# Routed feed-forward stage of a fused attention and expert layer: places given out in units of 128 in place of 256

## The chip, the cores and the metric

The kernel runs on one core of a Trainium2 chip. The metric is the device time of one execution in microseconds; every time here is of that core. PE is TensorE, DVE is VectorE, ACT is ScalarE, POOL is GpSimd, SP is SyncE, which issues most of the transfers.

## What is computed

For 4096 rows of 256 numbers (8 batches of 512), in float32:

```python
xn = layernorm(x)
attn = differential_attention(xn)        # 16 heads, two softmaxes each, output projection, layer norm
logits = xn @ switch_w + switch_b        # 8 experts
route, prob = argmax(logits), max(softmax(logits))
ffn[t] = prob[t] * (gelu(xn[t] @ w1[e] + b1[e]) @ w2[e] + b2[e])   # e = route[t], w1 256x1024, w2 1024x256
out = x + attn + ffn
```

Each row needs the feed-forward of one expert only, and how many rows an expert gets is known only on the chip.

## The kernel before

There are two stages, each a block in which every engine has its own instruction list and engines wait for each other through semaphores.

**Front stage** (`front_stage`, lines 109 to 1100). After the layer norm, 64 pairs of heads (8 batches times 8 pairs) are worked through in 512 steps of 8 to a pair: scores on PE, maximum on DVE (L872), exponential on ACT (L621), scaling on POOL (L468), combination on DVE (L839), transposes (L1012) and the product with V (L1027) on PE. The switch logits come out beside the V projections.

**Routing.** The generator `routing` (from L700) holds the plan as 27 small DVE operations; `ROUTE_OPS` says how many are slipped in behind each step from step 452. They find each row's expert, count the rows of each expert, and give every row a place: an expert gets whole tiles of 256 places (`FFN_TILE`). So 23 tiles (5888 places) cover every way in which 4096 rows can fall to 8 experts. L751 to L767 turn counts into tiles, the end of each expert's tiles (`tile_end`) and its first place (`base`); L789 to L799 say which expert each tile has (`tile_expert`). Places are turned into a table place to token with one-hot matrices: 24 of 32 are made by POOL (one to a step from step 476), 8 by DVE (one every third step), and 32 small matmuls (L1040) in the last pair join them. Places that no row holds get token 0 and are computed too.

**Feed-forward and output stage** (`ffn_and_output_stage`, from L1144). Matrices are split into a high and a low part, and each product is three matmuls (`THREE`) on operands of type float32r. Every engine goes through 23 turns, one for each tile n: turns 0 to 2 unrolled, 18 in a hardware loop, 2 unrolled (`turns`). Turn n:
- PE (`body`, L1668): the hidden layer of tile n, 48 matmuls with w1 as weights and 256 places moving (L1647), in four groups of 12; 4 transposes of tile n+1 (L1633); then the output of tile n-1, 48 matmuls (L1662), in which 128 places are the weights and the 256 columns of w2 move, once for each half of the tile.
- ACT (L1425): for each of the four groups two Gelus (L1435) and a copy as high part (L1438); the high part of tile n+1's rows (L1422); the high part of w2 (L1445).
- DVE (L1505): the low part of each group (L1522), among them the high part (L1490, two halves) and the low part (L1494, two halves) of w1 for tile n+1; the low part of tile n+1's rows (L1482); bias and eviction of tile n-1's output (L1502).
- POOL (L1379): fetches the rows of tile n+2 with two indirect transfers (L1137), then the low part of w2 of tile n (L1386), which waits for ACT's high part.
- SP (L1283): loads w1 of tile n+2, w2 of tile n+1 (1 MB each, always, also if the expert is the same), their biases, and stores tile n-1's output (L1305), which waits for DVE.

PE begins the hidden layer of tile n+1 only when L1494 and L1482 for it are done (lines 1639 and 1640). For the last tile the low part of w2 is split between POOL and DVE (L1559), after DVE's eviction of the tile before. SP issues the first loads of the output stage in the last turn; the later ones stand in its list behind the wait for the last tile's store. The output stage then projects 16 groups of 256 rows (L1689), fetches each row's feed-forward result by its place (L1401, which waits for all stores), normalises and adds on DVE (L1554 to L1613), and stores.

Of the kernel before, what the change touches and what calls it, by code (L numbers as in the profile page):

```python
# [30 lines left out]
T = B * S  # L31
# [25 lines left out]
SC = SLOTS // P  # L57

# [43 lines left out]
def front_stage(nc, ins, wp_d, xn_d, oW_d, oP_d, consts, slot_u, prob, tile_expert, token, ahead, s_ost):  # L102
# [3 lines left out]
    with ExitStack() as ctx:  # L106
# [18 lines left out]
        with ExitStack() as early:  # L125
            exr, oh, inc, exc, ones, col, den, line, column, column_u, high_hot, low_hot0, marks, _, low_hot1 = (
                early.enter_context(nc.sbuf_tensor(name, shape, U32 if name == "column_u" else F32))
                for name, shape in (
# [39 lines left out]
        tiles, tile_end, base = sb("tiles", [P, NE]), sb("tile_end", [P, NE]), sb("base", [P, NE])  # L168
# [493 lines left out]
        def _(dve):  # L662
# [35 lines left out]
            def routing():  # L698
# [89 lines left out]
                fe = [P, FFN_TILES, NE]  # L788
                step(vec.tensor_tensor(past, tile_end[:, :].unsqueeze(1).to_broadcast(fe),  # L789
                                       consts[:, C_T:C_T + FFN_TILES].unsqueeze(2).to_broadcast(fe), ALU.is_le))  # L790
                yield
# [977 lines left out]
```

## Time and profile before

| what | us |
|---|---|
| runs of the kernel before: median of 3 (lowest, highest) | 1867.96 (1867.92, 1871.78) |
| profiled execution, its own time | 1870.38 |
| its span in the trace | 1868.6 |
| PE busy, of the span | 1809.5 (97%) |
| DVE busy | 1552.2 (83%) |
| ACT busy | 1416.2 (76%) |
| POOL busy | 706.8 (38%) |

Times in rows are microseconds from the start of the span unless marked ns; a line of a timeline gives the start, the time that a run of like instructions took together, the engine, the line of code, output<-inputs, the shape and the count, and in brackets the idle time of the engine before it with what ended it. "PEld" is PE's loading of weights, which overlaps its matmuls.

### The profile page before, as it was taken

To read this page: it belongs to the slowest core of one execution; us is meant where nothing else is said; L and a number is where in the kernel's file an instruction comes from. 1 tells how busy PE (TensorE), PEld (TensorE's weight loads), DVE (VectorE), ACT (ScalarE), POOL (GpSimd) and SP (SyncE) were. 2 spreads that over 40 slices of the span, in tenths; PEclk is the share of its full clock that TensorE was granted. 3 is DMA by queue.
4 is the path that set the end of the run, shared out by engine and by line. 5 is a ranking of instruction groups with operands and counts; after the bars stand their busy time and mean duration, and the time that the engine had idled before them with its cause. 6 is when DMAs were issued, how large, how long until landed. Compare 5 with 4: busy or idle time off the path is not lost. (4 is left out here: it accounts for less than half of the span.)

```text
span 1868.6 us, 33187 instructions
## 1 busy us (share of the span) xinstructions
PE 1809.5 (97%) x10656; PEld 1411.6 (76%) x10656; DVE 1552.2 (83%) x2562; ACT 1416.2 (76%) x3307; POOL 706.8 (38%) x789
## 2 busy tenths in 40 slices
PE   5899999999999999999999999999999999999896
PEld 4677777777777777777777777777777799999896
DVE  7888888888888888888888888889998776666488
ACT  6898888888888888888888888888788776666311
POOL 4444222333333222333333323232266455555443
PEclk9999999999999999999999999999999999999999
DMA  9998888888888888888888888888787686676797
GB/s 311 265 243 231 238 225 218 218 229 214 215 221 229 222 214 224 228 210 208 227 224 220 216 227 227 216 218 224 208 204 180 217 294 234 238 236 208 252 325 231
DMA packets 214133, 429.33 MB, mean 230 GB/s; under 512 B 28193, under 2 KB 108961, under 8 KB 207969
## 3 DMA queue, kind: packets, MB, share of 16 engines
q1 hardware_dynamic: 208960, 413.09, 79.6%
q0 software_dynamic: 5024, 14.42, 2.6%
q8 instruction: 74, 1.21, 0.3%
q14 instruction: 75, 0.61, 0.1%
HBM read 176.02 MB, written 50.07 MB: 121 GB/s over the span
## 5 line engine op out<-in xcount | busy, mean ns | idle before, releaser
L621 ACT ACTIVATE e<-p_score,nmax 128x512 f32<-128x512 f32 x1024 | 697.4, 689 | 129.3 <-DVE nmax L872 128.8
L872 DVE TENSOR_REDUCE nmax<-p_score 128x2 f32<-128x1024 f32 x512 | 623.8, 1218 | 168.5 <-PE p_score L1000 167.3
L468 POOL TENSOR_SCALAR e<-e,rrec,lam 128x512 f32<-128x512 f32 x512 | 394.0, 769 | 945.1 <-DVE rrec L832 944.9
L1000 PE MATMUL p_score<-ks,qs 128*128 128x512 f32 x2048 | 578.8, 404 | 8.6 <-DMA ks<-k_parts 7.6
L1000 PEld LDWEIGHTS p_score<-ks,qs 128*128 128x128 f32 x2048 | 365.1, 188 | 177.9 <-ACT e L621 52.3
L839 DVE SCALAR_TENSOR_TENSOR pm<-e,rrec 128x512 f32<-128x512 f32 x512 | 394.5, 771 | 0.4 <-POOL e L468 0.2
L963 PE MATMUL p_proj<-xh,w 128*128 128x512 f32 x1024 | 385.9, 418 | 6.0 <-POOL xl L446 4.6
L553 ACT COPY pT<-p_tr 128x512 f32<-128x512 f32 x512 | 301.1, 588 | 112.3 <-PE p_tr L1012 111.9
L1012 PEld LDWEIGHTS p_tr<-consts,pm 128*128 128x128 f32 x2048 | 249.2, 140 | 80.8 <-issue 19.5
L1012 PE MATMUL p_tr<-consts,pm 128*128 128x128 f32 x2048 | 308.3, 273 | 1.7 <-ACT pT L553 1.5
L1027 PE MATMUL p_pv<-pT,v 128*64 128x512 f32 x1024 | 247.7, 605 | 0.7 <-ACT pT L553 0.7
L963 PEld LDWEIGHTS p_proj<-xh,w 128*128 128x128 f32 x1024 | 194.3, 190 | 41.2 <-issue 6.5
L621 ACT ACTIVATION_READ_ACCUMULATOR e<-p_score,nmax 128x1 f32 x1024 | 205.9, 201 | 0.0
L963 PE MATMUL p_proj<-xl,w 128*128 128x512 f32 x512 | 202.0, 394 | 0.0
L1662 PE MATMUL p_y<-w2p,hp 128*128 128x256 f32 x1104 | 137.7, 284 | 2.6 <-DVE w2p L1559 2.6
L1386 POOL TENSOR_TENSOR w2p<-w,w2p 128x2048 fp32r<-128x2048 f32 (+1 forms) x22 | 99.6, 4526 | 106.0 <-ACT w2p L1445 106.0
L1662 PEld LDWEIGHTS p_y<-w2p,hp 128*128 128x128 f32 x1104 | 133.6, 191 | 2.8 <-DVE w2p L1559 2.8
L1027 PEld LDWEIGHTS p_pv<-pT,v 128*64 128x64 f32 x1024 | 62.1, 136 | 95.9 <-issue 95.0
L1435 ACT ACTIVATE h<-p_h,b 128x256 f32<-128x256 f32 x184 | 76.8, 468 | 75.9 <-PE p_h L1647 75.9
L1647 PE MATMUL p_h<-xsp,w1p 128*128 128x256 f32 x1104 | 130.1, 277 | 2.6 <-ACT h L1435 2.1
L1647 PEld LDWEIGHTS p_h<-xsp,w1p 128*128 128x128 f32 x1104 | 127.7, 188 | 3.6 <-ACT h L1435 2.3
L963 PEld LDWEIGHTS p_proj<-xl,w 128*128 128x128 f32 x512 | 98.0, 191 | 11.7
(177 smaller groups left out, 1863.7 us busy)
## 6 DMA issues: line engine op xcount, KB each, us to landing
ks<-k_parts SPq DMA_DIRECT2D x512, 256.0 KB, 4.6
qs<-q_parts SPq DMA_DIRECT2D x512, 128.0 KB, 4.4
w<-weight_parts_scratch SPq DMA_DIRECT2D x56, 1024.0 KB, 10.0
w<-in_w SPq DMA_DIRECT2D x46, 1024.0 KB, 7.8
oT_parts_scratch<-oT SPq DMA_DIRECT2D x32, 512.0 KB
op<-oT_parts_scratch SPq DMA_DIRECT2D x32, 512.0 KB
wv<-weight_parts_scratch SPq DMA_DIRECT2D x56, 256.0 KB, 5.4
weight_parts_scratch<-w SPq DMA_DIRECT2D x8, 1024.0 KB, 5.7
```

Of the source, the lines that this page charges most:

```text
L468: nc.gpsimd.tensor_scalar(e2, e2, rrec[:, g % 4, 1:2], lam[:, 0:1], ALU.mult, ALU.mult).then_inc(s_e2, 1)
L553: nc.scalar.copy(pT[pair % 2][st // QT][:, :, qt * P:(qt + 1) * P], p_tr[:, :, :]).then_inc(s_pT, 1)
L621: nc.scalar.activation(ex[:, g % EX, m, :], p_score[g % 2][:, m, :], ACT.Exp, bias=nmax[:, g % 2, m:m + 1], accum_out=rsum[:, g % 4, m:m + ...
L839: vec.scalar_tensor_tensor(out=pm[:, g % 4, :], in0=ex[:, g % EX, 0, :], scalar=rrec[:, g % 4, 0:1], in1=ex[:, g % EX, 1, :], op0=ALU.mult ...
L872: vec.tensor_reduce(nmax[:, g % 2, :], p_score[g % 2][:, :, :], AXX, ALU.max, negate=True).then_inc(s_max, 1)
L963: last_op = nc.tensor.matmul(bank[:, :], weights(j, a, what[0], u, k), x_part(batch, b, k, 0, S), start=(k == 0 and c == 0), stop=(k == KT ...
L1000: last_op = nc.tensor.matmul(p_score[g % 2][:, m, :], qs[j][u][:, m, qt * P:(qt + 1) * P], ks[j][u][:, m, part, :], start=(part == 0), sto ...
L1012: last_op = nc.tensor.transpose(p_tr[:, k, :], pm[:, g % 4, k * P:(k + 1) * P], ident)
L1027: last_op = nc.tensor.matmul(p_pv[u * D:(u + 1) * D, :], v[it % 2][:, k, c:c + D], pT[j][u][:, k, :], start=(k == 0), stop=(k == QT - 1))
L1386: nc.gpsimd.tensor_tensor(w2p[j][:, 1, 0:f, :], w2[j][:, 0:f, :], w2p[j][:, 0, 0:f, :].bitcast(F32), ALU.subtract).then_inc(s_w2lo, 1)
L1647: last_op = nc.tensor.matmul(p_h[g % 2][:, f % 2, :], w1p[j][:, a, k, f * P:(f + 1) * P], xsp[j][:, b, k, :], start=(k == 0 and c == 0), s ...
L1662: last_op = nc.tensor.matmul(p_y[j][:, s, :], hp[j][:, a, f, s * P:(s + 1) * P], w2p[j][:, b, f, :], start=(f == 0 and c == 0), stop=(f == ...
```

## The change

An expert now gets places in units of 128. There are 16 tiles of 256 places (`PAIR_TILES`) and 7 of 128 (`HALF_TILES`), 4992 places in all. The plan gives an expert pairs of units first, as long as there are wide tiles, and its remaining units in narrow ones; that takes 42 DVE operations in place of 27. Tiles 16 to 22 are narrow: their transposes, Gelus, splits, stores and fetches are half as wide; the hidden matmuls have 128 moving columns in place of 256, and the output matmuls are 24 in place of 48. The loop over turns runs over 10 tiles in place of 18, and the last 10 turns are unrolled in place of 2. POOL makes 20 one-hot matrices and DVE 12 (every second step from step 480). The diff, cut to its core (between the operations of the plan the lines `yield` and `ready()`, a wait for the operation before, are left out; twelve of the new ones are 8 elements wide):

```diff
-FFN_TILES = (T + NE * (FFN_TILE - 1)) // FFN_TILE
-SLOTS = FFN_TILES * FFN_TILE
+PAIR_TILES, HALF_TILES = T // FFN_TILE, NE - 1
+FFN_TILES = PAIR_TILES + HALF_TILES
+PAIR_SLOTS = PAIR_TILES * FFN_TILE
+SLOTS = PAIR_SLOTS + HALF_TILES * P
+def width(n):
+
+    return FS if n < PAIR_TILES else 1
...
-ROUTE_OPS = (1,) * 8 + (0, 0, 2) + (1,) * 17
-ONE_HOTS_FROM, HOT_FIRST = 476, 4
-POOL_HOTS = 24
+ROUTE_OPS = (1,) * 8 + (0, 0, 2, 1) + (2,) * 8 + (1,) * 6 + (2,) * 2 + (1,) * 5
+ONE_HOTS_FROM, HOT_FIRST = 480, 4
+POOL_HOTS = 20
...
-                em = [P, NE, MAXT]
-                step(vec.tensor_tensor(more, inc[:, :, NT - 1:NT].to_broadcast(em),
-                                       consts[:, C_J:C_J + MAXT].unsqueeze(1).to_broadcast(em), ALU.is_gt))
-                step(vec.tensor_reduce(tiles[:, :], more, AXX, ALU.add))
-                step(vec.tensor_tensor_scan(tile_end[:, :], ones[:, 0:NE], tiles[:, :], 0.0, ALU.mult, ALU.add))
-                step(vec.tensor_tensor(base[:, :], tile_end[:, :], tiles[:, :], ALU.subtract))
-                step(vec.tensor_scalar(base[:, :], base[:, :], float(FFN_TILE), None, ALU.mult))
-                step(vec.tensor_tensor(lg[:, :, :], lg[:, :, :], base[:, :].unsqueeze(1).to_broadcast(tne), ALU.add))
+                count = inc[:, :, NT - 1:NT]
+                dve.wait_ge(s_marks, 16)
+                eu, ep = [P, NE, NT], [P, NE, PAIR_TILES]
+                step(vec.tensor_tensor(units_of, count.to_broadcast(eu),
+                                       marks[:, M_UNIT:M_PAIR].unsqueeze(1).to_broadcast(eu), ALU.is_gt))
+                step(vec.tensor_reduce(units[:, :], units_of, AXX, ALU.add))
+                step(vec.tensor_tensor(pairs_of, count.to_broadcast(ep),
+                                       marks[:, M_PAIR:MARKS].rearrange("p (e j) -> p e j", j=PAIR_TILES), ALU.is_gt))
+                step(vec.tensor_reduce(pairs[:, :], pairs_of, AXX, ALU.add))
+                step(vec.tensor_tensor_scan(pair_end[:, :], ones[:, 0:NE], pairs[:, :], 0.0, ALU.mult, ALU.add))
+                step(vec.tensor_scalar(pair_stop[:, :], pair_end[:, :], float(PAIR_TILES), None, ALU.min))
+                step(vec.tensor_tensor(pair_base[:, :], pair_end[:, :], pairs[:, :], ALU.subtract))
+                step(vec.scalar_tensor_tensor(out=less[:, :], in0=pair_base[:, :], scalar=float(PAIR_TILES),
+                                              in1=pair_stop[:, :], op0=ALU.min, op1=ALU.subtract))
+                step(vec.scalar_tensor_tensor(out=singles[:, :], in0=less[:, :], scalar=float(FS), in1=units[:, :],
+                                              op0=ALU.mult, op1=ALU.add))
+                step(vec.tensor_scalar(singles[:, :], singles[:, :], 0.0, None, ALU.max))
+                step(vec.tensor_tensor_scan(single_end[:, :], ones[:, 0:NE], singles[:, :], 0.0, ALU.mult, ALU.add))
+                step(vec.tensor_scalar(limit[:, :], less[:, :], -float(FFN_TILE), None, ALU.mult))
+                step(vec.tensor_tensor(single_at[:, :], single_end[:, :], singles[:, :], ALU.subtract))
+                step(vec.tensor_scalar(single_at[:, :], single_at[:, :], float(P), float(PAIR_SLOTS), ALU.mult, ALU.add))
+                step(vec.tensor_tensor(single_at[:, :], single_at[:, :], limit[:, :], ALU.subtract))
+                step(vec.scalar_tensor_tensor(out=shift[:, :], in0=pair_base[:, :], scalar=float(FFN_TILE),
+                                              in1=single_at[:, :], op0=ALU.mult, op1=ALU.subtract))
+                step(vec.tensor_tensor(exr[:, :, :], lg[:, :, :], limit[:, :].unsqueeze(1).to_broadcast(tne), ALU.is_lt))
+                step(vec.tensor_tensor(exr[:, :, :], exr[:, :, :], shift[:, :].unsqueeze(1).to_broadcast(tne), ALU.mult))
+                step(vec.tensor_tensor(lg[:, :, :], lg[:, :, :], single_at[:, :].unsqueeze(1).to_broadcast(tne), ALU.add))
+                step(vec.tensor_tensor(lg[:, :, :], lg[:, :, :], exr[:, :, :], ALU.add))
...
-                if g >= ONE_HOTS_FROM and (g - ONE_HOTS_FROM) % 3 == 0:
-                    c = POOL_HOTS + (g - ONE_HOTS_FROM) // 3
+                if g >= ONE_HOTS_FROM and (g - ONE_HOTS_FROM) % 2 == 0:
+                    c = POOL_HOTS + (g - ONE_HOTS_FROM) // 2
...
+        LOOP_END = PAIR_TILES // 2 - 2
-                with engine.Fori(1, LOOPED // 2 - 1) as i:
+                with engine.Fori(1, LOOP_END) as i:
-                for n in (FFN_TILES - 2, FFN_TILES - 1):
+                for n in range(2 * LOOP_END + 1, FFN_TILES):
...
-                                    p_h[g % 2][:, f % 2, :], w1p[j][:, a, k, f * P:(f + 1) * P], xsp[j][:, b, k, :],
+                                    p_h[g % 2][:, f % 2, 0:t.fs * P], w1p[j][:, a, k, f * P:(f + 1) * P],
+                                    xsp[j][:, b, k, 0:t.fs * P],
...
-                for s in range(FS):
+                for s in range(fs):
...
-                        nc.scalar.activation(h[:, g, c, :], p_h[g % 2][:, c, :], ACT.Gelu_apprx_tanh,
+                        nc.scalar.activation(h[:, g, c, 0:t.fs * P], p_h[g % 2][:, c, 0:t.fs * P], ACT.Gelu_apprx_tanh,
...
-                    v.tensor_tensor(hp[j][:, 1, 2 * g:2 * g + 2, :], h[:, g, :, :],
+                    v.tensor_tensor(hp[j][:, 1, 2 * g:2 * g + 2, 0:t.fs * P], h[:, g, :, 0:t.fs * P],
...
-            add_b2(FFN_TILES - 1, 0, LOOPED // 2, False)
+            add_b2(FFN_TILES - 1, 0, LOOPED // 2, False, 1)
```

The loads of w1 and w2, their splits and every wait stay as they are.

## Rows read from the trace of the kernel before

**Rows 1.** Busy time by stretch: PE, PEld, DVE, ACT, POOL; clock, DMA share, GB/s.
```profile
1511.00:1738.00 227.00, 227.00 (x1952) 227.00 (x1951) 142.67 (x192) 153.64 (x273) 126.31 (x54) 1.00 0.71 236
```
**Rows 2.** The chain that ended last, one turn of the feed-forward stage.
```profile
1517.74 5.44 PE p_h L1647 x48
1523.18 0.44 PE p_x L1633 x4
1523.62 5.75 PE p_y L1662 x48
```
**Rows 3.** Timeline of PE near the end of the front stage.
```profile
1443.63 0.60 PE L1012 MATMUL p_tr<-consts,pm 128*128 128x128 f32 x4
1444.16 1.94 PE L1027 MATMUL p_pv<-pT,v 128*64 128x512 f32 x8
1447.49 1.88 PE L1040 MATMUL p_proj<-high_hot,low_hot 128*128 128x46 f32 x16
```
**Rows 4.** Timeline of ACT, DVE and POOL in the turn that begins at 1517.6.
```profile
1520.66 0.69 DVE L1522 TENSOR_TENSOR hp<-h,hp 128x512 fp32r<-128x512 f32 x1 [2.00 <-ACT hp L1438]
1521.27 0.69 DVE L1490 CAST w1p<-w 128x1024 fp32r<-128x1024 f32 x1
...
1523.32 0.83 ACT L1435 ACTIVATE h<-p_h,b 128x256 f32<-128x256 f32 x2
...
1524.06 1.22 DVE L1494 TENSOR_TENSOR w1p<-w,w1p 128x1024 fp32r<-128x1024 f32 x1
1524.18 0.62 ACT L1438 CAST hp<-h 128x512 fp32r<-128x512 f32 x1
...
1524.71 0.58 ACT L1422 CAST xsp<-p_x 128x512 fp32r<-128x512 f32 x1
1525.18 1.91 ACT L1445 CAST w2p<-w 128x2048 fp32r<-128x2048 f32 x1
1525.19 0.68 DVE L1522 TENSOR_TENSOR hp<-h,hp 128x512 fp32r<-128x512 f32 x1
1525.80 1.22 DVE L1494 TENSOR_TENSOR w1p<-w,w1p 128x1024 fp32r<-128x1024 f32 x1
1526.93 0.68 DVE L1482 TENSOR_TENSOR xsp<-p_x,xsp 128x512 fp32r<-128x512 f32 x1
1527.17 4.62 POOL L1386 TENSOR_TENSOR w2p<-w,w2p 128x2048 fp32r<-128x2048 f32 x1 [4.39 <-ACT w2p L1445]
```
**Rows 5.** Groups of DVE instructions, 1290 to 1440: busy us, mean ns.
```profile
L238 DVE TENSOR_SCALAR high_hot<-marks,column,consts 128x46 f32<-128x46 f32 x8 | 2.4, 302 | 0.0
L237 DVE TENSOR_SCALAR low_hot<-marks,line 128x128 f32<-128x128 f32 x8 | 2.2, 280 | 0.0
...
L767 DVE TENSOR_TENSOR lg<-lg,base 128x256 f32<-128x256 f32 x1 | 0.4, 418 | 0.0
...
L764 DVE TENSOR_SCALAR base<-base 128x8 f32<-128x8 f32 x1 | 0.2, 159 | 0.0
```
**Rows 6.** Timeline: DVE instructions that meet a POOL instruction.
```profile
1501.53 4.65 POOL L1386 TENSOR_TENSOR w2p<-w,w2p 128x2048 fp32r<-128x2048 f32 x1 [4.40 <-ACT w2p L1445]
...
1504.33 2.13 DVE L1543 TENSOR_SCALAR rows<-rows 128x512 f32<-128x512 f32 x1
```
**Rows 7.** Timeline of the last turn (begins 1726.8) and the start of the output stage.
```profile
1736.16 2.41 POOL L1386 TENSOR_TENSOR w2p<-w,w2p 128x1024 fp32r<-128x1024 f32 x1 [6.57 <-ACT w2p L1445]
...
1738.96 1.91 DVE L1559 TENSOR_TENSOR w2p<-w,w2p 128x1024 fp32r<-128x1024 f32 x1
...
1740.93 6.01 PE L1662 MATMUL p_y<-w2p,hp 128*128 128x256 f32 x48 [2.61 <-DVE w2p L1559]
...
1752.35 0.68 DVE L1502 TENSOR_TENSOR y<-p_y,b 128x512 f32<-128x512 f32 x1
```
**Rows 8.** Busy time of single pairs of heads: 54 (no routing) and 57.
```profile
1239.80:1261.80 22.00, 22.00 (x118) 15.94 (x117) 19.63 (x31) 18.31 (x46) 7.24 (x10) 1.00 0.92 238
...
1306.50:1330.00 23.50, 22.20 (x117) 15.94 (x115) 22.20 (x47) 18.79 (x46) 6.16 (x8) 1.00 0.76 203
```

More of the change, by code:

```diff
@@ L167, in front_stage @@
         sw, swb, weight = sb("sw", [P, KT, NE]), sb("swb", [P, NE]), sb("weight", [P, NE])
-        tiles, tile_end, base = sb("tiles", [P, NE]), sb("tile_end", [P, NE]), sb("base", [P, NE])
+        units, pairs, pair_end, pair_stop, pair_base, less, singles, single_end, limit, single_at, shift = (
+            sb(name, [P, NE]) for name in ("units", "pairs", "pair_end", "pair_stop", "pair_base", "less", "singles",
+                                           "single_end", "limit", "single_at", "shift"))
         te_f = sb("te_f", [P, FFN_TILES])
@@ L787, in routing @@
                 yield
[L788 to L791, printed above, removed]
+                for ends, a, b in ((pair_end, 0, PAIR_TILES), (single_end, PAIR_TILES, FFN_TILES)):
+                    fe = [P, b - a, NE]
+                    step(vec.tensor_tensor(past[:, a:b, :], ends[:, :].unsqueeze(1).to_broadcast(fe),
+                                           consts[:, C_T + a:C_T + b].unsqueeze(2).to_broadcast(fe), ALU.is_le))
+                    yield
                 ready()
@@ L1135, in gather @@
     def gather(self, pool, n, s):
-        c = n * FS + s
+        c = n * FS + s if n < PAIR_TILES else PAIR_TILES * (FS - 1) + n
         pool.indirect_dma_start(
@@ L1242, in __init__ @@
                 self.half_before = half - 1 if j == 0 else half
+                self.fs, self.fs_next, self.fs_before = (width(n + d) if exact else FS for d in (0, 1, -1))
             def after(self, k):
@@ L1294, in body @@
                 if t.after(1):
-                    store(n - 1, 1 - j)
+                    store(n - 1, 1 - j, t.fs_before)
                 if t.has(1):
@@ L1301, in body, with store @@
                     first_of_output()
-            def store(n, j):
+            def store(n, j, fs):
                 sp.wait_ge(s_yb, n + 1)
-                sp.dma_start(ys_v[bass.ds(n, 1)].rearrange("a p s e -> (a p) s e"), y[j][:, :, :]
-                             ).then_inc(s_st[j], 16)
+                if fs == 1:
+                    a = PAIR_SLOTS + (n - PAIR_TILES) * P
+                    sp.dma_start(ys_d[a:a + P, :], y[j][:, 0, :]).then_inc(s_st[j], 16)
+                else:
+                    sp.dma_start(ys_v[bass.ds(n, 1)].rearrange("a p s e -> (a p) s e"), y[j][:, :, :]
+                                 ).then_inc(s_st[j], 16)
             x_v = ins["x"].rearrange("(n s p) e -> n p s e", s=2, p=P)
@@ L1347, in _ @@
             load_whole(2)
-            store(FFN_TILES - 1, 0)
+            store(FFN_TILES - 1, 0, 1)
             def store_out(n):
@@ L1375, in gather @@
                 pool.wait_ge(s_tr, n - 1)
-                for s in range(FS):
+                for s in range(width(n)):
                     ahead.gather(pool, n, s)
@@ L1417, in _, with x_high @@
         def _(act):
-            def x_high(n, j, fresh):
+            def x_high(n, j, fresh, fs):
                 act.wait_ge(s_tr, n + 1)
@@ L1495, in w1_low, with add_b2 @@
                                 ALU.subtract).then_inc(s_w1lo, 1)
-            def add_b2(n, j, half, fresh):
+            def add_b2(n, j, half, fresh, fs):
                 dve.wait_ge(s_y, n + 1)
@@ L1537, in body @@
                 if t.after(1):
-                    add_b2(n - 1, 1 - j, t.half_before, not t.after(3))
+                    add_b2(n - 1, 1 - j, t.half_before, not t.after(3), t.fs_before)
             assert HG == 2 * KT
@@ L1626, in _, with transposes @@
         def _(pe):
-            def transposes(n, j, half, fresh):
-                pe.wait_ge(s_xs[j], 16 * FS * (half + 1))
+            def transposes(n, j, half, fresh, fs):
+                pe.wait_ge(s_xs[j], 16 * FS * (half + 1) if fs == FS else 16 * (PAIR_TILES // 2 * (FS - 1) + half + 1))
                 if not fresh:
@@ L1631, in transposes @@
                 for k in range(KT):
-                    for s in range(FS):
+                    for s in range(fs):
                         last_op = nc.tensor.transpose(p_x[j][:, k, s * P:(s + 1) * P],
@@ L1651, in hidden, with outputs @@
                     if g == X_AT and t.first():
-                        transposes(1, 1, 0, True)
-            def outputs(n, j, fresh):
+                        transposes(1, 1, 0, True, FS)
+            def outputs(n, j, fresh, fs):
                 pe.wait_ge(s_w2lo, n + 1)
@@ L1658, in outputs @@
                     pe.wait_ge(s_yb, n - 1)
-                for s in range(FS):
+                for s in range(fs):
                     for f in range(FT):
@@ L1669, in body @@
                 if t.has(1) and not t.first():
-                    transposes(t.n + 1, 1 - t.j, t.half_next, not t.after(1))
+                    transposes(t.n + 1, 1 - t.j, t.half_next, not t.after(1), t.fs_next)
                 if t.after(1):
-                    outputs(t.n - 1, 1 - t.j, not t.after(3))
+                    outputs(t.n - 1, 1 - t.j, not t.after(3), t.fs_before)
             turns(body)(pe)
             pe.wait_ge(s_w2lo_dve, 1)
-            outputs(FFN_TILES - 1, 0, False)
+            outputs(FFN_TILES - 1, 0, False, 1)
             pe.wait_ge(s_wohi, 4)
```

75 lines of the change are left out of this document (52 added, 23 removed).

## The prediction

> **What bounds the kernel now.** I read the busy time by stretch first. In the feed-forward stretch PE is busy in 227.0 of 227.0 us and nothing else is near it: ACT 154, DVE 143, POOL 126, the transfers 0.71 of their time, clock 1.00 [rows 1]. Then the chain of waits: a turn is PE alone, 5.44 us of hidden layer, 0.44 of transposes, 5.75 of output, in sum 11.63 [rows 2]. So work taken from PE here shortens the kernel until something else in the turn ends last, and the question is what. For that I read one turn's timeline [rows 4] and the places where DVE and POOL meet [rows 6, 7]. Last, the front stage by pairs of heads, for the longer plan [rows 8].
>
> **Part 1: PE in a narrow turn.** The output matmuls keep their shape and half of them go: 24 of 48, 5.75/2 = 2.88 us saved. Two of four transposes go: 0.22 saved [rows 2]. The hidden matmuls stay 48, with 128 columns in place of 256; today one takes 5.44/48 = 0.113. No row shows a float32r matmul of 128 columns. Bounds: half of today, 0.057, and, from the other end, the pace of plain float32 products, where 4 matmuls of 512 columns take 1.94 us (8 records), 0.24 for 128 columns [rows 3]. The nearest rows are the transposes, with 128 columns: 0.44/4 = 0.11 each [rows 2], the same in the front stage; and 16 products of only 46 columns take 1.88, 0.117 each [rows 3]: with fresh weights for each matmul, fewer columns don't get below about 0.11. I take 0.108: 48 give 5.2, a saving of 0.25. A narrow turn is then 5.2 + 0.22 + 2.88 = 8.3 us for PE, 3.3 less.
>
> **Part 2: what else must fit into it.** Times from the start of the turn's hidden layer. ACT: today two Gelus take 0.83 and the high copy 0.62, and the last copy is over at 1524.8, 7.2 after the turn's start: 5.44 of hidden layer, 0.83, 0.62 and 0.3 on the way [rows 2, 4]. Half the width takes DVE from 0.68 to 0.42 [rows 4, 5], about 1 ns a column; so the two Gelus become 0.63 and the copy 0.40. The last copy is then over at 5.2 + 0.3 + 0.63 + 0.40 = 6.5, the rows' copy at 6.8, and w2's copy, unchanged at 1.9 [rows 4], at 8.7. POOL's split of w2 (4.62 [rows 4], unchanged) can run from 8.7 to 13.3, that is to 4.6 of the next turn. Today it starts 2.0 before the turn's end and is over 2.6 into the next one, before DVE's first low part at 3.1 [rows 4].
> In a narrow turn the two meet, and rows show what a meeting costs. A DVE operation of 512 columns that started inside POOL's split took 2.13 us, until 1506.46, while the split ended at 1506.18 [rows 6]: it waited for the whole instruction. Another of 1024 took 1.91 beside POOL against 1.22 alone [rows 4, 7]. The Trainium skill (page "SBUF — State Buffer", section "Who interferes with whom") states it as a rule against such a change: DVE with two inputs in SBUF, or in a two-port mode, and GpSimd lock each other out for a whole instruction. By that rule the turn below is 9.5, without it 8.7.
> So DVE and POOL take turns. DVE's share of a narrow turn: four low parts (0.61 apart today [rows 4], 0.34 at half width), two w1 copies at 0.61 and two w1 splits at 1.13 (1524.06 to 1525.19 [rows 4]): 1.36 + 1.22 + 2.26 = 4.84. POOL's is 4.65. Sum **9.5**, against PE's 8.3. (Today 4.65 + 2.44 + 3.48 = 10.6 fits into 11.63.) PE's wait: the next hidden layer needs the split of w1 and the rows' low part, the last of DVE's list. I take 9.5 for a turn in this rhythm.
> Lower bound 8.7: no lock, DVE's list alone (last copy at 6.5, low part, split, rows' low part: 0.34 + 1.13 + 0.41 and waits). Upper bound 10.6: POOL starts before DVE's last split, so that this one waits too.
> Transfers: today 236 GB/s [rows 1] in 11.63 us are 2.74 MB a turn; the narrow store and fetch take off 0.26. That is 2.48 MB in 9.5 us, 261 GB/s, and a share of 0.71 x 2.48/2.74 x 11.63/9.5 = 0.79. SP's load of w2 for the next tile waits for POOL's split, now until 4.2 in the turn, and ACT needs it at 6.8 of the next, 12 us later; today's two loads of a turn fit into 11.63. I cost them at nothing; without this cover the turn would grow to what keeps the share under 1, 7.5 us, still less. The turns that leave the loop cost nothing either: the front stage is unrolled and PE stays busy in 22.0 of 22.0 us [rows 8].
>
> **Part 3: turns 15 to 22.** Before: 7 turns of 11.63 (15 to 21) = 81.4. After: turn 15 loses two transposes, 11.4; 16 has a narrow hidden layer but the wide output of tile 15, 5.2 + 0.22 + 5.75 = 11.2; in 17 POOL is done at 2.1 and DVE is not held up, 8.7; in 18 POOL is busy to 4.6 and DVE has 4.84 and the rows' 0.42 to go, 9.9; 19 to 21 at 9.5, 28.5. Sum 69.7, **saved 11.7**.
> Last turn: before, PE starts tile 22's output 14.1 after the turn's start (1740.93 - 1726.8) and is done at 19.9, with 2.61 of waiting for DVE's half of w2 [rows 7]. After: outputs of 21 end at 8.1; ACT's w2 copy ends at 8.4, POOL's half (2.41 [rows 7]) at 10.9, and DVE's half, two SBUF inputs, waits for it and needs 1.22: 12.1, and the output 2.88 more, 15.0. The stall grows from 2.6 to 4.0 and the whole is 4.9 shorter. The output stage behind it runs on loads that SP issues after the last store, which follows DVE's eviction at 1752.35 [rows 7], 25.6 after the turn's start; that eviction stands behind the third group's load, which waits for the same split. It moves by about 4.4. **Saved 4.4**, the smaller.
>
> **Part 4: the plan.** Removed: 0.42 + 0.16 x 3 + 0.28 x 2 = 1.5 us of DVE. Added, by size from rows 5: six of 256 columns at 0.42, two of 128 at 0.28, twelve of 8 at 0.16: 5.0. Four more one-hot matrices at 0.28 + 0.30: 2.3. Together 5.8 more on DVE over five pairs of heads. Lower bound 0: a pair without routing leaves DVE 22.0 - 19.6 = 2.4 idle. Upper bound 5.8. In the pair with the densest routing of today DVE had 2.6 us more to do and the pair took 1.5 longer, PE idle for 1.3 of it [rows 8], which holds also the waits for PE's rank matmuls. New steps hold two operations each, the second waiting for the first. I take **1.2 lost**. POOL's one-hots are four fewer, and end in the same step. DVE's wait for the marks moves up, to step 464, with the maximum L872 and so ACT's exponential behind it; their load is issued 16 steps (two pairs, 44 us) before, and I cost it at nothing.
>
> **Sum.** -11.7 - 4.4 + 1.2 = -14.9. The profiled execution took 1870.4 (span 1868.6): 1855.5. The median of the runs is 2.4 lower, 1867.96: **1853.1**.
>
> **Rivals.**
> (a) DVE and POOL don't line up as said, or the lock doesn't bind: 8.7 a turn in 18 to 21 saves 3.6 more, and the last turn 1.1: 1848. For it: DVE's first low part needs to slip past POOL's split only once. Against: rows 6.
> (b) A worse rhythm, or PE's clock: with PE waiting 1.2 us in each turn and its array half filled, the clock may go to its lower level, 1.2 GHz; then 24 output matmuls cost 2.88 more, 11.2 a turn. Either, 10.6 to 11.2 for five turns, plus a plan that costs 2 or 3: 1858 to 1863. Against: PE's clock stayed at 1.00 through the pair with 1.3 us of idling [rows 8].
> (c) Slower: a float32r matmul of 128 columns goes at the pace of float32, 0.24 each: the hidden layer takes 11.6, a narrow turn 14.7. Turns 16 to 21 then cost 6 + 5 x 3.1 = 21.5 more, the end 1.7 more, the plan 1.2: 1892. It decides from where PE's gain is used up, 21.6 us / (7 x 48) = 0.064 above today's 0.113, so 0.18 a matmul. For it: nothing in the kernel has this form under 256 columns. Against: the transposes.
> (d) The plan gives no fewer tiles: excluded, the number of turns and widths is fixed in the program.
>
> **Chances.** Forecast (1850 to 1856) 0.5, (a) 0.2, (b) 0.2, (c) 0.05, the rest (a plan or a front stage that eats the gain) 0.05. A measurement of this kernel tells about 0.2%, 3.7 us, from no change. Below 1864.2 lie the first three, nearly all of (b): faster 0.91, the same 0.03, slower 0.06. The range leaves out (c) and the end of (b): 1846.5 to 1860.
>
> **What would show it.** In the trace after, narrow hidden matmuls at 5.2 us for 48 (near 2.7: rows 3 misled; near 11: (c)); turns 19 to 21 at 9.5, with PE waiting about 1.2 for DVE's L1482 or L1494; DVE's first low part in these turns longer than 1 us, ending when POOL's split ends (if all stay near 0.42, no lock: (a)); before the last output a wait of 4; pairs 58 to 62 together about 1 us longer. Wrong in kind if PE stays without waits in narrow turns or the clock of that stretch falls below 1.

## The result and the profile after

| | median us | lowest to highest | runs |
|---|---|---|---|
| before | 1868.76 | 1867.92 to 1871.78 | 4 |
| after | 1853.72 | 1851.60 to 1859.52 | 4 |

The ratio on record is 0.9909, 95% interval 0.9891 to 0.9928; the quotient of the two medians is 0.9920, inside it. By the medians the change is 15.0 us faster, where 14.9 and 1853.1 us had been forecast. The profiled execution of the new kernel is the slowest of its four, 1859.52 us (span 1857.7), 6 us above the median. So these rows show something that not every execution has, and the agreement of the medians says nothing yet about the steps.

Line numbers have moved: the hidden layer is L1712 on PE, the transposes L1698, the output L1728; w2's low part is L1450 on POOL and its last half L1624 on DVE; DVE's low parts are L1586 (groups) and L1546 (rows), w1's copy and split L1554 and L1558, the eviction L1566; ACT's copy of w2 is L1509.

Busy time by stretch, each row about one turn, turns 16 to 22 and the last outputs (columns as in [rows 1]; the digits before DMA share and GB/s are PE's granted clock):

```profile
1659.50:1670.80 11.30, 11.30 (x100) 11.30 (x100) 6.11 (x10) 6.21 (x14) 6.41 (x3) 1.00 0.71 231
1670.80:1679.30 8.50, 8.41 (x74) 8.20 (x73) 6.15 (x11) 6.20 (x14) 2.83 (x2) 1.00 0.67 179
1679.30:1689.10 9.80, 8.71 (x75) 8.51 (x75) 7.33 (x11) 6.20 (x14) 6.47 (x3) 1.00 0.98 353
1689.10:1702.50 13.40, 13.40 (x76) 13.40 (x77) 6.73 (x10) 6.19 (x14) 6.36 (x3) 0.62 0.61 201
1702.50:1711.00 8.50, 8.44 (x75) 8.23 (x73) 6.22 (x11) 6.20 (x14) 4.15 (x2) 1.00 0.72 247
1711.00:1720.80 9.80, 8.69 (x74) 8.48 (x74) 7.33 (x11) 6.21 (x15) 5.50 (x2) 1.00 0.52 177
1720.80:1732.90 12.10, 8.55 (x73) 8.35 (x73) 6.19 (x8) 6.77 (x14) 7.55 (x3) 0.96 0.75 233
1732.90:1738.40 5.50, 5.50 (x26) 5.50 (x27) 4.35 (x2) 1.05 (x1) 5.50 (x4) 0.50 1.09 360
```

In [rows 1] PE filled its stretch. Here it is full in turn 16, lacks 1.1 us in turns 18 and 21, and in turn 19 is full again for 13.4 us with the very same work: the clock was 0.62 of full speed on average.

The chain of waits, turn 16 and parts of turns 18 and 19 (for [rows 2]):

```profile
1659.49 5.31 PE p_h L1712 x48
1664.80 0.24 PE p_x L1698 x2
1665.04 5.76 PE p_y L1728 x48
...
1682.14 0.04 DVE hp L1586
1682.18 1.95 issue
...
1686.08 0.29 DVE w1p L1558
1686.37 0.78 issue
...
1688.61 0.42 DVE xsp L1546
1689.03 0.04 issue
1689.08 8.79 PE p_h L1712 x48
1697.86 0.45 PE p_x L1698 x2
```

Before, a turn's chain was PE alone. Now turn 18's runs over DVE, and the long piece of "issue" in it, 1.95 us, lies inside DVE's L1586. The timeline says what it is (for [rows 4, 6]):

```profile
1679.32 5.58 PE L1712 MATMUL p_h<-xsp,w1p 128*128 128x128 f32 x48
1679.36 4.56 POOL L1450 TENSOR_TENSOR w2p<-w,w2p 128x2048 fp32r<-128x2048 f32 x1 [5.58 <-ACT w2p L1509]
...
1682.14 2.06 DVE L1586 TENSOR_TENSOR hp<-h,hp 128x256 fp32r<-128x256 f32 x1 [2.47 <-ACT hp L1502]
1684.73 0.41 DVE L1586 TENSOR_TENSOR hp<-h,hp 128x256 fp32r<-128x256 f32 x1
...
1688.15 4.95 POOL L1450 TENSOR_TENSOR w2p<-w,w2p 128x2048 fp32r<-128x2048 f32 x1 [3.11 <-ACT w2p L1509]
1689.08 8.79 PE L1712 MATMUL p_h<-xsp,w1p 128*128 128x128 f32 x48 [1.07 <-DVE xsp L1546]
```

POOL's split runs to 1683.92. The DVE instruction that began at 1682.14 ends at 1684.20; its like alone takes 0.41. It stood still until POOL was done, and all that follows it on DVE is late, down to the rows' low part for which PE waits 1.07 us.

The last turn (for [rows 7]; it begins at 1720.81):

```profile
1729.37 0.42 DVE L1566 TENSOR_TENSOR y<-p_y,b 128x256 f32<-128x256 f32 x1 [1.40 <-PE p_y L1728]
1729.39 2.34 POOL L1450 TENSOR_TENSOR w2p<-w,w2p 128x1024 fp32r<-128x1024 f32 x1 [4.55 <-ACT w2p L1509]
1729.71 3.10 DVE L1624 TENSOR_TENSOR w2p<-w,w2p 128x1024 fp32r<-128x1024 f32 x1
...
1732.87 5.49 PE L1728 MATMUL p_y<-w2p,hp 128*128 128x256 f32 x24 [3.54 <-DVE w2p L1624]
```

DVE's half of w2 again sits out POOL's half, and PE waits 3.54 us. The 24 outputs then take 5.49 us, at the lower level of the clock (0.50, so 1.2 GHz).

The routing, pair 57 and the sum over pairs 56 to 62 (for [rows 8]):

```profile
1307.30:1330.70 23.40, 22.13 (x117) 15.92 (x115) 22.14 (x47) 18.71 (x46) 6.15 (x8) 1.00 0.77 204
...
sum 157.20, PE 155.58 PEld 112.62 DVE 146.49 ACT 129.13 POOL 68.23; mean PE 22.23 PEld 16.09 DVE 20.93 ACT 18.45 POOL 9.75
```

The same seven pairs took 157.3 before, with 142.8 of DVE. DVE does 3.7 us more and the pairs take no longer.

### The profile page after: what moved, and what is told of

The parts are those of the page before. It is cut to its first block and busy times, and to the rows that moved or that the text cites. A ratio compares the mean times of both kernels' runs of the same rounds, so it can differ in the third digit from the quotient of the medians.

```text
span 1857.7 us, 32559 instructions
## 1 busy us (share of the span) xinstructions
PE 1795.7 (97%) x10474; PEld 1397.3 (75%) x10474; DVE 1549.6 (83%) x2585; ACT 1405.4 (76%) x3307; POOL 693.7 (37%) x774
## 5 line engine op out<-in xcount | busy, mean ns | idle before, releaser
L1450 POOL TENSOR_TENSOR w2p<-w,w2p 128x2048 fp32r<-128x2048 f32 (+1 forms) x22 | 99.9, 4542 | 107.9 <-ACT w2p L1509 107.9
L1712 PE MATMUL p_h<-xsp,w1p 128*128 128x256 f32 (+1 forms) x1104 | 134.5, 283 | 4.9 <-DVE xsp L1546 2.2
L1712 PEld LDWEIGHTS p_h<-xsp,w1p 128*128 128x128 f32 x1104 | 132.0, 195 | 6.8 <-DVE xsp L1546 3.2
L1499 ACT ACTIVATE h<-p_h,b 128x256 f32<-128x256 f32 (+1 forms) x184 | 70.9, 436 | 79.6 <-PE p_h L1712 78.7
L1728 PE MATMUL p_y<-w2p,hp 128*128 128x256 f32 x936 | 121.4, 290 | 3.5 <-DVE w2p L1624 3.5
L1728 PEld LDWEIGHTS p_y<-w2p,hp 128*128 128x128 f32 x936 | 117.2, 197 | 3.7 <-DVE w2p L1624 3.7
L1586 DVE TENSOR_TENSOR hp<-h,hp 128x512 fp32r<-128x512 f32 (+1 forms) x92 | 61.1, 668 | 55.6 <-ACT hp L1502 36.0
```

The source lines that it names most:

```text
L1450: nc.gpsimd.tensor_tensor(w2p[j][:, 1, 0:f, :], w2[j][:, 0:f, :], w2p[j][:, 0, 0:f, :].bitcast(F32), ALU.subtract).then_inc(s_w2lo, 1)
L1712: last_op = nc.tensor.matmul(p_h[g % 2][:, f % 2, 0:t.fs * P], w1p[j][:, a, k, f * P:(f + 1) * P], xsp[j][:, b, k, 0:t.fs * P], start=(k = ...
L1728: last_op = nc.tensor.matmul(p_y[j][:, s, :], hp[j][:, a, f, s * P:(s + 1) * P], w2p[j][:, b, f, :], start=(f == 0 and c == 0), stop=(f == ...
```

## The experiments

They settle three things: what the plan costs; whether it is POOL's split that holds the narrow turns above 8.7; and what turn 19's 13.3 us are. Lengths of turns below are from one start of the hidden layer to the next. The kernel before ran beside each group of experiments: its median is 1873.04 us beside experiments 1 to 4, 1866.67 beside 5 to 8 and 1866.92 beside 9 to 11. So times of different groups are compared by their ratios.

**1. The plan alone.** The new routing, but all 23 tiles computed at full width.

```diff
-                self.fs, self.fs_next, self.fs_before = (width(n + d) if exact else FS for d in (0, 1, -1))
+                self.fs, self.fs_next, self.fs_before = (FS, FS, FS)
...
-                for s in range(width(n)):
+                for s in range(FS):
```

> The longer plan and the 23 tiles of the change, with tiles 16 to 22 computed at full width: the second half of a narrow tile fetches the same rows again and is not stored. Theory (the plan hides in DVE's idle time): within 0.1% of the kernel before, turns 15 to 22 as before, 11.6 each. Rival (the plan costs what I forecast): 1.2 us longer; at the bound of all of DVE's added work on the path, 5.8 longer.

Measured: 1870.86 us against 1873.04, ratio 0.9994 (0.9981 to 1.0007). The plan costs nothing that can be told from this, at most 1.3 us (which does not exclude the 1.2 of the forecast), and the gain comes from the narrow tiles. In the trace the turns from 15 on are 11.63 to 11.70.

**2. The change again.**

> The changed kernel once more, for more rounds and a second trace. Its profiled execution was 6 us longer than its three other runs, and in its trace the clock was at its lower level for 10 us in turn 19 and again at the last output. Theory (the clock falls by chance in narrow turns, after PE has waited about 1 us for DVE): the place of the fall differs in this trace or it is missing; the time is 1851 to 1860, ratio 0.991. Rival (the slow stretch is a fixed trait of the code): the same fall in turn 19, 13.4 us for that turn.

Measured: 1855.31 us, ratio 0.9908 (0.9894 to 0.9923). Turn 19 takes 13.28 in this profile too, with the clock at its lower level from about 1692.1 on. From two profiles I took this fall for a fixed trait of the kernel. Experiment 9 shows that it isn't.

**3. Hidden matmuls of a narrow tile with 256 moving columns.** The 128 surplus columns are old numbers that nobody reads.

```diff
-                                    p_h[g % 2][:, f % 2, 0:t.fs * P], w1p[j][:, a, k, f * P:(f + 1) * P],
-                                    xsp[j][:, b, k, 0:t.fs * P],
+                                    p_h[g % 2][:, f % 2, :], w1p[j][:, a, k, f * P:(f + 1) * P],
+                                    xsp[j][:, b, k, :],
```

> The hidden matmuls of the narrow tiles get 256 moving columns back; the second 128 hold what an earlier tile left there and nothing reads their results. All else stays narrow. Theory (a matmul with fresh weights costs about 0.11 whether 128 or 256 columns move, and the turn is set by DVE and POOL): narrow turns stay at 8.5 and 9.5 to 9.8; PE's array is full again, so the clock does not fall, and the time is as the fastest runs of the changed kernel or better, ratio 0.989 to 0.991. Rival (the halved columns do bring time): 1 to 2 us slower than the changed kernel. Rival (the clock falls because PE waits, whatever the columns): a fall like that in the changed kernel.

Measured: 1853.93 us, ratio 0.9909 (0.9892 to 0.9925), the same as the change on that chip. Turns 17 to 21: 8.81, 9.83, 9.22, 9.75, 9.23. Busy time by stretch, turns 18 to 20:

```profile
1677.70:1687.50 9.80, 8.99 (x75) 8.78 (x75) 7.21 (x11) 6.21 (x14) 6.24 (x3) 1.00 0.95 366
1687.50:1696.70 9.20, 9.00 (x74) 8.80 (x74) 6.52 (x11) 6.21 (x14) 5.06 (x3) 1.00 0.74 273
1696.70:1706.50 9.80, 9.05 (x75) 8.85 (x75) 7.12 (x11) 6.21 (x14) 6.21 (x3) 1.00 0.74 247
```

PE is busy 9.0 of a turn in place of 8.7: twice the columns for 0.3 us. The turn doesn't follow, since PE isn't what it is made of. The clock stayed up in turns 16 to 21 of this one profile, which at the time looked like the work of the wide matmuls. But of this kernel's six executions one without a profile took 1860.30 us at a mean granted clock of 0.989; those of the change in which the clock fell have 0.988.

**4. A short POOL.** In tiles 16 to 21 POOL makes an eighth of w2's low part; the rest is left out. DVE and every wait stay.

```diff
-                j, f = n % 2, HALF_F if n == FFN_TILES - 1 else FT
+                j, f = n % 2, HALF_F if n == FFN_TILES - 1 else FT if n < PAIR_TILES else 1
```

> For tiles 16 to 21 POOL makes only an eighth of the low part of w2 (one of 8 slices); the rest of it is left out. Every wait stays. Theory (DVE's two-input instructions wait for POOL's whole instruction): DVE's first low part in turns 18 to 21 takes 0.42 in place of 1.5 to 2.1, PE's waits of about 1.1 us in turns 19 and 22 go, the five narrow turns 17 to 21 take 8.5 each, 2 to 3 us less in all than the changed kernel with its clock up. Rival (DVE's list is too long by itself): the turns stay at 9.5 to 9.8 and only the last stall shrinks.

Measured: 1852.60 us, ratio 0.9892 (0.9874 to 0.9910). That interval overlaps the one of the change (0.9894 to 0.9923), so what follows rests on the trace and not on the time. Turns 18 to 21 of its timeline are 8.79, 8.79, 8.79, 8.80:

```profile
1691.37 5.58 PE L1712 MATMUL p_h<-xsp,w1p 128*128 128x128 f32 x48
1691.41 0.73 POOL L1450 TENSOR_TENSOR w2p<-w,w2p 128x256 fp32r<-128x256 f32 x1 [6.94 <-ACT w2p L1509]
...
1694.20 0.43 DVE L1586 TENSOR_TENSOR hp<-h,hp 128x256 fp32r<-128x256 f32 x1 [2.47 <-ACT hp L1502]
```

POOL is out of the way 2 us before DVE's first low part, which takes 0.43 in place of 1.5 to 2.1. Without POOL on the port a narrow turn is 8.8; so the lock is what the rest of the turn is made of. The transfers, at 0.90, 0.85, 0.88 and 0.60 of their time in these four turns, hold nobody up: PE is busy 8.7 of 8.8.

**5. POOL's split in four pieces**, so that DVE can slip in between.

```diff
+                pieces = 4 if PAIR_TILES <= n < FFN_TILES - 1 else 1
+                for a in range(0, f, f // pieces):
+                    b = a + f // pieces
+                    last_op = nc.gpsimd.tensor_tensor(w2p[j][:, 1, a:b, :], w2[j][:, a:b, :],
+                                                      w2p[j][:, 0, a:b, :].bitcast(F32), ALU.subtract)
```

> POOL's low part of w2 of tiles 16 to 21 is cut into four instructions of 512 columns; the same work. Theory (DVE waits for one whole instruction at a time, and the port time of both adds up to 9.5 a turn): DVE's first low part in a late narrow turn waits for at most 1.2, but later ones wait too, so a turn stays at 9.3 to 9.8. Rival (what costs is where the one long wait falls, not the sum): the turns fall to 8.8 as with the shortened POOL instruction.

Measured: 1853.59 us against 1866.67, ratio 0.9931 (0.9908 to 0.9953). Turn 18 takes 10.04, turns 20 and 21 9.14 and 9.57, turn 19 13.30 with the clock down. Timeline, turn 18:

```profile
1678.67 5.17 POOL L1453 TENSOR_TENSOR w2p<-w,w2p 128x512 fp32r<-128x512 f32 x4 [4.86 <-ACT w2p L1513]
1681.45 1.25 DVE L1590 TENSOR_TENSOR hp<-h,hp 128x256 fp32r<-128x256 f32 x1 [2.47 <-ACT hp L1506]
1682.62 1.77 DVE L1558 CAST w1p<-w 128x1024 fp32r<-128x1024 f32 x1
```

DVE's long wait of 2.06 has become two, and POOL's four pieces wait as well (5.17 in place of 4.56). Cutting the instruction changes who waits when, not the sum. The copy waits too (1.77 against 0.68), though it reads one input.

**6. DVE makes w2's low part** in the narrow tiles: alone it needs 2.28 us for what takes POOL 4.57.

```diff
-                if n == 0:
+                if n == 0 or n >= PAIR_TILES:
                     continue
...
+                if t.exact and PAIR_TILES <= n < FFN_TILES - 1:
+                    dve.wait_ge(s_w2lo, n)
+                    dve.wait_ge(s_w2hi, n + 1)
+                    v.tensor_tensor(w2p[j][:, 1, :, :], w2[j][:, :, :], w2p[j][:, 0, :, :].bitcast(F32),
+                                    ALU.subtract).then_inc(s_w2lo, 1)
```

(and the last tile's first half behind the last turn)

> For tiles 16 to 22 DVE makes the low part of w2 in place of POOL, after the eviction in its list. DVE needs 1.13 for 1024 columns where POOL needs 2.3, so by my sum the shared port is in use 4.84 + 2.26 = 7.1 a turn in place of 9.5, and DVE 7.8 of PE's 8.3. Theory: no long low parts, turns 17 to 21 at 8.8 each, the last output starts 11.0 after turn 22's start in place of 12.1, no fall of the clock in turn 19; 3 to 6 us faster than the changed kernel, ratio 0.987 to 0.989. POOL's additions for the output stage move into turns 20 and 21 and may hold DVE up there for up to 1.2 at a time. Rival (DVE, not the port, is what the narrow turns lack): the turns stay at 9.5 or grow.

Measured: 1857.19 us, ratio 0.9953 (0.9939 to 0.9967): a miss, slower than the change by the ratios (0.9908 and 0.9927 in experiments 2 and 9). Turns 18 to 21 are 8.79, 14.19, 14.39, 8.69. Two are as forecast; the timeline shows the other two:

```profile
1693.90 6.62 DVE L1558 TENSOR_TENSOR w1p<-w,w1p 128x1024 fp32r<-128x1024 f32 x1
1694.48 4.94 POOL L1455 TENSOR_TENSOR x<-x,rows 128x512 f32<-128x512 f32 x4
...
1700.90 10.50 PE L1719 MATMUL p_h<-xsp,w1p 128*128 128x128 f32 x48 [5.50 <-DVE xsp L1546]
```

POOL's list, free of the splits, went on to the output stage: its four additions of beta, which had stood behind the last split, now ran in turn 19. One DVE split of 1.22 stood still through all four of them. The forecast had put these additions into turns 20 and 21 and allowed for a hold of 1.2 at a time. PE waited 5.50, its clock fell in that wait, at about 1699.8, and the next 48 hidden matmuls took 10.50.

**7. The same with 256 moving columns.**

> As dve_w2, with 256 moving columns in the hidden matmuls of the narrow tiles, of which the second half is not used. Theory (half-filled matmuls matter only for the clock, and with PE hardly waiting it does not fall anyway): as dve_w2 within 0.1%, each hidden layer 0.1 longer. If the clock falls in dve_w2 and not here, the columns decide.

Measured: 1857.62 us, ratio 0.9951 (0.9938 to 0.9965). Turns 18 to 21: 9.07, 14.45, 11.23, 9.07, the same accident. The clock fell here too, at about 1698.1, in the same wait: wide matmuls don't keep it up through that.

**8. Narrow and wide tiles in turn** (narrow in turns 10, 12 to 22, hidden matmuls with 256 columns), so that a wide turn covers POOL's split. The core of the edit:

```diff
-    return FS if n < PAIR_TILES else 1
+    return 1 if n >= FIRST_HALF and (n - FIRST_HALF) % 2 == 0 else FS
```

> The narrow tiles are turns 10, 12, ... 22 in place of 16 to 22, wide ones between them; POOL makes w2's low part; hidden matmuls with 256 columns. Theory (port time adds up over neighbouring turns): a narrow and a wide turn need 9.5 + 10.65 = 20.15 of the port and 20.2 of PE, so a pair takes 20.2 to 20.6 where the changed kernel takes 11.63 + 9.3 = 20.9: 2 to 4 us faster in the stretch of turns 10 to 22 than hidden256. Rival (the wide turn with a narrow output, 8.5 for PE, can't hold its own 10.65 of port time next to its neighbour): pairs of 21 or more, nothing gained.

Measured: 1857.19 us, ratio 0.9953 (0.9938 to 0.9969): nothing gained. Turns alternate between 11.95 and 9.96, 21.9 a pair:

```profile
1675.40:1687.40 12.00, 11.96 (x101) 11.96 (x102) 6.61 (x10) 6.35 (x14) 7.73 (x3) 1.00 0.64 219
1687.40:1697.40 10.00, 8.79 (x77) 8.59 (x75) 7.29 (x11) 7.61 (x14) 4.76 (x4) 1.00 0.73 265
```

A wide turn of 11.63 and a narrow one of 9.4 would make 21.0. The first kind of turn (narrow hidden layer, wide output) is PE alone. The second (wide hidden layer, narrow output) has PE busy for 8.8 of 10.0, and the timeline says what it waits for:

```profile
1690.61 0.69 DVE L1598 TENSOR_TENSOR hp<-h,hp 128x512 fp32r<-128x512 f32 x1 [2.33 <-ACT hp L1514]
...
1697.35 2.86 PE L1724 MATMUL p_h<-xsp,w1p 128*128 128x256 f32 x22 [1.21 <-DVE xsp L1558]
```

POOL's split had ended at 1689.46. From 1690.61 to 1697.30 DVE works through its list with hardly a gap, and no instruction in it takes longer than it does alone (0.69, 1.22, 0.42). So this turn's 9.96 is 3.2 us until the first low part and 6.7 of DVE's own list, and not time on the port. The rival's outcome came true, but not for the rival's reason, and the sum of port times of a pair, 20.15, was not what set its length.

The results of this kernel are wrong, so it counts for its lengths only. By its code the likely reason is this: turn 8 is still in the loop and loads w1 and b1 for turn 10 as if that were wide tile 10, so the first narrow tile gets the hidden weights of another tile. The amount of work is the same.

**9. The change a third time**, beside the two that follow.

> The change once more, on the chip of the next two. Both theories: 0.991 of the time before, turns 17 to 21 at 8.7, 9.8, 13.3, 8.7, 9.8, last outputs 12.1 after the start of turn 22.

Measured: 1853.10 us against 1866.92, ratio 0.9927 (0.9914 to 0.9941). In this profile (1852.96 us) the clock stayed up. Turns 17 to 21: 8.69, 9.77, 9.18, 9.38, 9.19. Timeline of turns 19 to 22:

```profile
1688.81 5.58 PE L1712 MATMUL p_h<-xsp,w1p 128*128 128x128 f32 x48 [1.08 <-DVE xsp L1546]
...
1697.99 5.58 PE L1712 MATMUL p_h<-xsp,w1p 128*128 128x128 f32 x48 [0.50 <-DVE xsp L1546]
1700.82 1.67 DVE L1586 TENSOR_TENSOR hp<-h,hp 128x256 fp32r<-128x256 f32 x1 [2.55 <-ACT hp L1502]
...
1707.37 5.58 PE L1712 MATMUL p_h<-xsp,w1p 128*128 128x128 f32 x48 [0.70 <-DVE xsp L1546]
...
1716.56 5.61 PE L1712 MATMUL p_h<-xsp,w1p 128*128 128x128 f32 x48 [0.51 <-DVE xsp L1546]
```

PE's wait before turn 19, 1.08, is that of the first profile to 0.01 us, and the 48 matmuls behind it take 5.58 here and 8.79 there. So the fall of the clock comes in some executions and not in others, with nothing in turns 17 and 18 to tell them apart, and costs 4.0 us over turns 19 to 21 (13.28 + 8.68 + 9.77 against 9.18 + 9.38 + 9.19). In the first profile a wait of 1.08 before turn 22 brought no fall either.

The same thing happens in turn 3, where all tiles are wide. There PE waits 2.06 to 2.09 us in the middle of the hidden layer in every profile. These are the rows of the first profile and of this one:

```profile
1509.18 4.63 PE L1712 MATMUL p_h<-xsp,w1p 128*128 128x256 f32 x24 [2.07 <-ACT h L1499]
...
1510.41 3.10 PE L1712 MATMUL p_h<-xsp,w1p 128*128 128x256 f32 x24 [2.07 <-ACT h L1499]
```

The clock falls behind this wait in 6 of the 13 profiles (experiments 1, 2, 6, 10 and 11 and the first of the change) and stays up in the other 7, the kernel before among them; the fall makes turn 3 15.6 us in place of 14.1. The first profile is 6.5 us longer than this one: 4.0 in turns 19 to 21, 1.5 in turn 3, 2.2 from the start of turn 22 to the end, less 1.2 ahead of turn 2. The first two profiles of the change have both falls and this one has neither; experiment 5 has the fall in turn 19 alone. Experiments 3 and 4 can't be read as cures of it: one profile each.

**10. DVE makes the splits, and POOL is held back.** Experiment 6 with one line more, ahead of POOL's additions of beta:

```diff
             pool.wait_ge(s_scaled, 1)
+            pool.wait_ge(s_w2lo_dve, 1)
             for n in range(R):
                 add_beta(n)
```

> GpSimd takes no w2 split from tile 16 on and is held back from its four additions of beta until the last tile's split is done, so that VectorE has the shared port to itself. Theory of the port: no turn has a long wait; turns 17 to 21 at 8.7 to 8.9 each, no fall of the clock in turn 19, last outputs 11.3 after the start of turn 22. From the turns of the two profiles the stretch is then 5 to 8 us shorter than with the change, about 1848 where the change has 1854; what the late additions of beta cost behind the last tile comes off that (at most their 4.9 us). Rival (VectorE itself becomes the bound, or the clock falls for the matmuls of 128 columns whatever waits): turns of 9.5 or more, or a turn of 13, and a time at or above the change's.

Measured: **1846.37 us** (1844.71 to 1849.41) against 1866.92, ratio **0.9887** (0.9872 to 0.9903), and 6.7 us under the change on the same chip, whose interval doesn't touch this one. Turns 17 to 21: 8.68, 8.79, 8.80, 8.79, 8.79. Busy time of turns 18 to 20, then of turn 22 and the last outputs:

```profile
1679.90:1688.70 8.80, 8.69 (x74) 8.49 (x74) 8.06 (x12) 6.21 (x14) 1.66 (x1) 1.00 0.93 325
1688.70:1697.50 8.80, 8.69 (x74) 8.48 (x74) 8.05 (x12) 6.22 (x14) 1.66 (x1) 1.00 0.84 300
1697.50:1706.30 8.80, 8.68 (x75) 8.48 (x75) 8.04 (x12) 6.21 (x14) 0.00 (x0) 1.00 0.84 290
...
1715.10:1726.40 11.30, 8.52 (x73) 8.31 (x73) 7.00 (x10) 6.78 (x14) 0.00 (x0) 1.00 0.77 234
1726.40:1729.50 3.10, 3.10 (x26) 3.10 (x27) 3.04 (x2) 1.06 (x1) 3.02 (x2) 1.00 1.01 316
```

DVE does 2.3 us more work in each turn, and the turn is shorter: PE is busy 8.7 of 8.8. The last outputs start 11.3 after their turn's start and take 3.1, the clock is up, and the late additions on POOL (6.88 us for four, beside DVE's first splits of the output stage) cost less than they free. Against the profile of experiment 9, turns 17 to 21 are 2.4 us shorter and the rest behind them 2.1, in sum 4.5. The 5 to 8 that were forecast for the stretch had been counted from two profiles with the fall in turn 19; against those the turns are 6.3 shorter. In the profiles the span is 3.6 shorter, since this one has the fall in turn 3. The medians say 6.7.

**11. The same with 256 moving columns.**

> The same with 256 moving columns in the hidden matmuls of the narrow tiles. Theory of the port: turns at 8.8 to 9.1, so 0 to 2 us above the kernel with 128 columns. If the clock needs the wide matmuls also where nobody waits, this one is faster than the one with 128 columns by 3 us or more.

Measured: 1849.83 us, ratio 0.9906 (0.9891 to 0.9921). Turns 18 to 21: 9.07, 9.06, 9.07, 8.90. The median is 3.5 us above experiment 10 where 0 to 2 were expected, but the intervals overlap and the profiles' spans differ by 0.9 only. Turns 17 to 21 together are 1.0 longer, and the last outputs 1.5, where this profile has a fall of the clock after PE's wait of 2.78 and that of experiment 10 has none after the same wait. Nothing speaks for the wide matmuls here.

## Why the prediction came out right, step by step

- **Narrow hidden layer, 5.2.** Right: 5.31 in the chain of turn 16. The row that carried it was the 46-column matmul at 0.117 each: half the columns save 2%, and rival (c), which needed 0.18 a matmul, falls. Outputs at half, 2.9, and transposes at 0.24: right.
- **DVE and POOL take turns, 9.5.** Right in mechanism and size. The Trainium skill's rule (page "SBUF — State Buffer", section "Who interferes with whom") is what the rows show: DVE's first low part takes 1.5 to 2.1 and ends just behind POOL's split, and with POOL shortened (experiment 4) the turn is 8.8. A lock for one whole instruction doesn't cover experiment 6, where a DVE split recorded ahead of POOL's first addition sat out all four. Turns 17 to 21 were forecast at 8.7, 9.9, 9.5, 9.5, 9.5, and in the undisturbed profile are 8.69, 9.77, 9.18, 9.38, 9.19. The mean of the last three is 9.25: the sum of port times was 0.25 too high. In turn 20 POOL's split takes 4.56 where 4.65 was put in, DVE's share from the end of that split (1702.21) to the end of its last w1 split (1706.98) is 4.77 where 4.84 was, and POOL's next split is recorded from 1706.83, 0.15 ahead of that end. PE's waits are 0.5 to 1.1 where about 1.2 was said.
- **Rival (a), no lock,** is refuted by experiments 4 and 10, which have that length of turn, 8.8, only where POOL is off the port.
- **Rival (b), the clock.** Priced at 0.2 and for five turns, it happens in part: in two of three profiles for one turn, 4.0 us each time. The argument against it, that the clock stayed up through 1.3 us of idling in the front stage [rows 8], didn't bear that weight. The forecast had named a clock below 1 in this stretch as a sign that it is wrong in kind; by that sign two profiles speak against it and one for it, although the lengths of the turns without the fall are as it said. This is the step that was weakest. Turn 3 shows that the narrow tiles aren't needed for such a fall. The two profiled executions that show it took 1859.5 and 1858.9 us, the one without it 1853.0; the medians of the change, 1853.7, 1855.3 and 1853.1, lie nearer to the latter. How often the fall comes without a profile isn't shown.
- **Turns 15 to 21, 69.7.** 68.98 in the undisturbed profile, 72.95 in the first (11.47 + 11.31 + 8.68 + 9.76 + 13.28 + 8.68 + 9.77). Saved against 81.4: 12.4 or 8.5, forecast 11.7.
- **Last turn.** Last outputs start 12.06 after the turn's start (12.1 forecast), after a wait of 3.54 (4.0). They take 5.49, not 2.88: the clock falls in this stall, in all three profiles, which the forecast didn't have. From the start of the turn to the end of the span it is 136.9 us in place of 141.7, so 4.8 saved where 4.4 was forecast, and 7.1 in the third profile (134.6). The forecast had let the output stage hang on SP's loads and not on these matmuls, and gave no working for its 4.4; neither was tested by itself. That the fall costs nothing at the end can't be said: experiments 10 and 11 have the same wait of 2.78, and the one with the fall takes 133.7 from the start of the turn to the end, the one without it 132.5.
- **The plan, 1.2.** Mis-sized: 0.0 in the pairs of the first profile; experiment 1 by itself only says no more than 1.3. The 3.7 us that DVE does more in seven pairs fell into its idle time. The forecast had priced the steps' density by pair 57, which is as long as before (23.4) with the same 22.1 of DVE: the new operations stand in other steps.
- **The sum.** For the third profile, by parts: 12.4 saved in turns 14 to 21 and 7.1 from there to the end, 2.0 lost ahead of turn 14, in sum 17.4. Of what is lost ahead, 0.7 to 2.0 us lie before turn 2 in the three profiles, against the one of before. Nothing ties them to the plan: in the nine experiments with other kernels, which all have the new plan, turn 2 starts anywhere from 0.7 earlier to 5.5 later than before. What makes that start move isn't explained. The profile of before and the third one are also not of the same group of runs: in its own group the third has a median 13.8 below the kernel before. The median of the first group, 15.0 saved, comes from four runs, one of them with the fall. So the forecast of 14.9 met it with a gain 2.5 smaller than the profile without those falls shows, and it had left the falls out. The mechanism was right; the closeness to the last microsecond was luck.

## What to carry to other kernels

When the bound engine's share of a turn is cut, add up what the engines behind it do on a shared resource as if it were one engine; here 4.84 of DVE and 4.65 of POOL gave 9.5 and measured 9.2 to 9.8. The sum is one bound among others: in experiment 8 it gave 20.15 for a pair of turns, and PE in one turn and DVE's own list in the other made 21.9. If the sum ends above the bound engine, give the work to the engine that holds the resource for less time, even the busier one (2.28 us in place of 4.57). And look at what else stands in the list of the engine that you free: its next work starts earlier, here on the same port, and cost 5.5 us until one wait held it back.

## What the runs showed of the hardware

- A DVE instruction can be shut out by more than one POOL instruction: of the four in a row in experiment 6 it sat out all, 6.62 us for 1.22 of work, though it is recorded as begun 0.58 ahead of the first. It ended 1.10 after the last of them. In experiment 5 a DVE instruction got in between the third and the fourth of four pieces (1.25 us, with the fourth piece at 1.47 in place of 1.27). What decides is not shown.
- PE's granted clock fell from 2.4 to 1.2 GHz while PE was working, 2 us after a wait of 1.07 had ended, and stayed there for 10.2 us; in another execution the same wait brought no fall. Behind a wait of 2.07 in turn 3, where the matmuls have 256 columns, it fell in 6 of 13 profiles, for about 3 us. In each narrow turn of experiment 10, where the weight loads waited 0.31 and the matmuls 0.1, it stayed up through the stretch, with 128 columns as well; in the long wait of experiments 6 and 7 it fell with 128 and with 256. Whether the width of the matmuls has any part in it stays open.
- A float32r matmul with fresh weights takes 0.113 us with 256 moving columns (5.44 for 48, rows 2) and 0.111 with 128 (5.31 for 48, turn 16 of the change).
